# Causal mask in the stack rows, maxima of a batch in one round, transposed scores four units later: two transformer layers with expert stages on one core

## The reference

```python
scores = jnp.einsum('bhqd,bhkd->bhqk', q, k) / jnp.sqrt(jnp.float32(D))
causal = jnp.tril(jnp.ones((T, T), dtype=bool))
scores = jnp.where(causal, scores, -jnp.inf)
weights = jax.nn.softmax(scores, axis=-1)
out = jnp.einsum('bhqk,bhkd->bhqd', weights, v)
```

## Time and profile before

| what | value |
|---|---|
| median of 3 runs | 541.39 us (540.93 to 545.23) |
| the profiled execution | 542.69 us, span 541.0 us |
| TensorE busy | 458.8 us, 85% |
| VectorE, ScalarE, GpSimd busy | 324.4, 247.3, 203.2 us |
| mean granted clock of TensorE | 0.938 |
| steps 1 and 2 | 34.4 to 75.8 us |
| layer-0 experts | 75.8 to 111.4 us |
| steps 3 to 11 | 111.4 to 298.7 us |
| steps 12 and 13 | 298.7 to about 364 us |
| layer-1 experts | about 370 to 449.9 us |
| steps 14 to 18 | 449.9 to 541 us |

### The profile page before, as it was taken

One profiled execution on the slowest core, in us unless ns is written; L12 is line 12 of the kernel. 1 busy time (PEld: TensorE's weight loads), 2 busy tenths in 40 slices (PEclk: granted clock), 3 DMA queues, 4 the chain that ended last, 5 costly groups with the idle time before them and its releaser, 6 DMA issues.

```text
span 541.0 us, 10168 instructions
## 1 busy us (share of the span) xinstructions
PE 458.8 (85%) x3431; PEld 344.6 (64%) x3431; DVE 324.4 (60%) x974; ACT 247.3 (46%) x564; POOL 203.2 (38%) x274
## 2 busy tenths in 40 slices
PE   1668899979899999989989965787999997978874
PEld 1645667656777877767656634456999995654442
DVE  5475631135777877778868964314666664564952
ACT  1821545535555564555445522323555554434542
POOL 6620110004335435435444366870000001767761
PEclk9999999989999999999999977866999998888968
DMA  5642224644314313202357120312222201322130
GB/s 157 155 123 62 71 52 119 189 116 120 94 33 122 110 37 99 76 6 79 124 113 228 46 75 28 124 44 64 60 59 80 73 23 35 107 67 81 35 90 21
DMA packets 51441, 45.89 MB, mean 85 GB/s; under 512 B 4968, under 2 KB 46464, under 8 KB 51392
## 3 DMA queue, kind: packets, MB, share of 16 engines
q1 hardware_dynamic: 47424, 35.54, 23.4%
q0 software_dynamic: 2240, 4.53, 3.1%
q10 hardware_dynamic: 1728, 5.20, 3.0%
HBM read 26.24 MB, written 19.01 MB: 84 GB/s over the span
## 4 chain that ended last, share of the span: by engine, by line
PE 57%; POOL 16%; DVE 8%; issue 8%; DMA 5%; ACT 5%; SPq 1%; ACTq 0%; POOLq 0%; DVEq 0%
PE ps_S L1493 6%; POOL xs L741 6%; PE ps_N L1468 5%; PE ps_N L1658 5%; PE ps_P L1512 5%; POOL PT L688 4%; PE ps_N L1464 4%; PE ps_P L1668 3%; PE ps_M L1709 3%; PE ps_M L1668 3%; PE ps_S L1658 2%; PE ps_M L1555 2%; PE ps_M L1592 2%; POOL XN L750 2%; POOL LATE L750 2%
## 5 line engine op out<-in xcount | busy, mean ns | idle before, releaser
L823 ACT ACTIVATE PT<-ps_S 128x512 f32<-128x512 f32 x192 | 112.3, 591 | 109.2 <-PE ps_S L1493 87.7
L1058 DVE TENSOR_REDUCE NM<-ps_N 128x2 f32<-128x512 f32 (+1 forms) x192 | 127.9, 682 | 51.3 <-PE ps_N L1468 40.0
L688 POOL TENSOR_SCALAR_AFFINE_SELECT PT<-PT 128x512 f32<-128x512 f32 x128 | 78.6, 639 | 172.6 <-ACT PT L823 171.9
L1468 PE MATMUL ps_N<-STK 96*128 96x256 f32 (+1 forms) x256 | 105.7, 456 | 0.0
L1493 PE MATMUL ps_S<-STK 100*128 100x128 f32 (+5 forms) x352 | 88.1, 327 | 17.1 <-ACT PT L823 13.5
L1493 PEld LDWEIGHTS ps_S<-STK 104*128 104x128 f32 (+1 forms) x352 | 62.3, 200 | 25.0 <-ACT PT L823 17.9
L1464 PE MATMUL ps_N<-maskb,identb 128*128 128x256 bf16 (+1 forms) x192 | 63.5, 331 | 11.4 <-issue 8.3
L1512 PE MATMUL ps_P<-PT,VA 128*32 128x256 f32 (+1 forms) x1024 | 59.7, 351 | 7.3 <-POOL PT L688 6.8
L1468 PEld LDWEIGHTS ps_N<-STK 96*128 96x128 f32 x256 | 53.4, 208 | 4.7 <-issue 0.7
L1512 PEld LDWEIGHTS ps_P<-PT,VA 128*32 128x32 f32 x1024 | 28.1, 114 | 36.8 <-issue 15.0
L730 POOL TENSOR_TENSOR ROT<-ROT 128x256 f32<-128x256 f32 (+1 forms) x16 | 11.3, 728 | 97.1 <-DVE ROT L1087 97.1
(11 more groups left out here) (195 smaller groups left out, 811.4 us busy)
## 6 DMA issues: line engine op xcount, KB each, us to landing
STK<-scr SPq DMA_DIRECT2D x96, 96.0 KB
scr<-XQ SPq DMA_DIRECT2D x24, 256.0 KB
ROT<-in_L_ffn_W SPq DMA_DIRECT2D x16, 256.0 KB, 3.0
EW<-in_moe ACTq DMA_DIRECT2D x8, 512.0 KB, 3.6
scr<-XQ SPq DMA_DIRECT2D x24, 128.0 KB
xs<-zero SPq DMA_DIRECT2D x1, 2496.0 KB, 11.1
LATE<-xs SPq DMA_DIRECT2D x9, 256.0 KB, 2.9
ysl<-LATE SPq DMA_DIRECT2D x9, 256.0 KB, 2.3
```

The source lines that it names most:

```text
L688: last = pool.affine_select(out=v, in_=v, compare_op=ALU.is_ge, fill=0.0, base=0, pattern=[[0, 4], [1, P]], channel_multiplier=-1)
L823: act.activation(PT[:, g, r, :], bank[s][:], ACT.Exp, scale=SCALE).then_inc(exp_ok, 1)
L1058: dve.tensor_reduce(NM[b % 2][:, h, qt, :].rearrange("q (p c) -> q c p", p=2)[:, slots[0]:slots[-1] + 1, :], bank[s][:].rearrange("q (c p ...
L1468: last = mm(s[:, 2 * w_ * i:2 * w_ * (i + 1)], stk[0:QK_ROWS, c, P * qt:P * (qt + 1)], stk[0:QK_ROWS, k_slots(L, c, 2 * h, 2), 0:w_], star ...
```

## The change

1. *Mask.* The natural scores no longer get a mask product. The key side of partitions 104 to 125 holds powers of two and the query side negative ones, so that the product of partitions 0 to 127 adds a large negative number wherever key is above query in the diagonal block (`CO_KM`, `CO_QM`; blocks of `MBLK` = 6 tokens). `constant_rows` writes partitions 96 to 127 of both sides with five activations a stack. A unit of the last 128 queries is now two matmuls (keys 0 to 127 over 96 rows, keys 128 to 255 over 128 rows). Since partitions 96 to 103 now take part in the natural product, they have to be zero on the query side when a stack is reused: SyncE copies zeros there, a ninth DMA of the load.
2. *Maxima.* `mxt`, `max_high`, `max_low`, `mrow` work once on 16 heads instead of twice on 8.
3. *Order.* `ST_AT` = 4: the transposed scores of batch c start in unit 4 of their step and reach into units 0 to 3 of the next. The other items move with them.

```diff
-WARM = [(), ()]
 QK_ROWS, ST_ROWS = 96, 104
+MBLK = 6
...
-        t[QK_ROWS + 2 * r:QK_ROWS + 2 * r + 2, CO_SEL + r] = 1.0
+        t[[QK_ROWS + r, QK_ROWS + 4 + r], CO_SEL + r] = 1.0
...
+    for i in range(P):
+        for j in range(-(-P // MBLK)):
+            row, at = ST_ROWS + j, i % MBLK
+            if i // MBLK == j:
+                t[row, [CO_KM + i, CO_KM + P + i]] = 2.0 ** (22 * at - 107)
+                if at < MBLK - 1:
+                    t[row, [CO_QM + i, CO_QM + P + i]] = -2.0 ** (103 - 22 * at)
+            elif i // MBLK < j:
+                t[row, [CO_QM + i, CO_QM + P + i]] = -2.0 ** 124
...
+            early = t == 0
+            if u == (0 if early else 2):
                 add("qk", a)
+            if a and u == (0 if early else 2 + a[0]):
                 add("hi", a)
-            if a and u == a[0]:
+            if a and u == (0 if early else 3 + a[0]):
                 add("lo", a)
...
-            add("st", c, u // 3, u % 3)
+            s, v = (c, u - ST_AT) if u >= ST_AT else (d, u + 12 - ST_AT)
+            add("st", s, v // 3, v % 3)
             add("max", b, u)
-            add("exp", c, u // 3, u % 3)
-            if u % 3 == 2:
-                add("msk", c, u // 3)
+            add("exp", s, v // 3, v % 3)
+            if v % 3 == 2:
+                add("msk", s, v // 3)
...
             if u == 0:
-                add("pv", d, 3)
+                add("mxt", c)
+                add("mrow", c)
+                add("pv", d, 0)
             if u == 1:
-                add("mxt", c, 1)
-                add("mrow", c, 1)
-                add("stack", a)
-                add("ocp", d, 1)
+                add("pv", d, 1)
             if u == 2:
-                add("val", a)
+                add("ocp", d, 0)
             if u == 3:
+                add("pv", d, 2)
+            if u == 4:
+                add("pv", d, 3)
+            if u == (1 if early else 5):
+                add("stack", a)
+            if u == (2 if early else 5):
+                add("val", a)
+            if u == 5:
+                add("ocp", d, 1)
+            if u == (3 if early else 6):
                 add("vev", a)
+            if u == 7:
                 add("otr", d)
                 add("norm", d)
...
-            if u == 5:
-                add("ott", d)
-                layer1("po", e)
-            if u == 6:
-                add("oev", d)
-                add("mxt", b, 0)
-                add("mrow", b, 0)
             if u == 7:
-                add("proj", d)
+                layer1("po", e)
             if u == 8:
-                add("res", d)
-                add("pv", c, 0)
...
             if u == 9:
-                add("pv", c, 1)
+                add("ott", d)
...
             if u == 10:
-                add("ocp", c, 0)
+                add("oev", d)
                 layer1("pl", e)
             if u == 11:
-                add("pv", c, 2)
+                add("proj", d)
+                add("res", d)
...
-            def ones_rows(i):
+            def constant_rows(i):
 
-                act.activation(STK[i][QK_ROWS:ST_ROWS, KS:, :].rearrange("x (c r) t -> x c r t", r=4),
-                               K[QK_ROWS:ST_ROWS, None, CO_SEL:CO_SEL + 4, None].broadcast_to((ST_ROWS - QK_ROWS, 4, 4, T)), ACT.Copy)\
-                    .then_inc(ones_ok, 1)
+                act.activation(STK[i][QK_ROWS:P, 0:KS, :], K[QK_ROWS:P, None, CO_QM:CO_QM + T].broadcast_to((P - QK_ROWS, KS, T)),
+                               ACT.Copy)
+                for r in range(4):
+                    last = act.activation(STK[i][QK_ROWS:P, KS:, :].rearrange("x (c r) t -> x r c t", r=4)[:, r],
+                                          K[QK_ROWS:P, None, CO_KM:CO_KM + T].broadcast_to((P - QK_ROWS, 4, T)), ACT.Identity,
+                                          bias=K[QK_ROWS:P, CO_SEL + r:CO_SEL + r + 1])
+                last.then_inc(ones_ok, 1)
...
-                sp.dma_start(scm[L][b][h], MS[h][:].bitcast(F32)).then_inc(scm_w[h], 16)
-                sp.wait_ge(scm_w[h], 16 * (seq(L, b) + 1))
-                for p in range(2):
-                    r = 2 * h + p
...
+                sp.dma_start(scm[L][b].rearrange("s h t -> h s t"), MS[:].bitcast(F32)).then_inc(scm_w, 16)
+                sp.wait_ge(scm_w, 16 * (n + 1))
+                sp.dma_start(STK[n % NSTK][QK_ROWS:ST_ROWS, 0:KS, :].bitcast(F32),
+                             scm[L][b].rearrange("s (r c) t -> (s r) c t", c=KS)).then_inc(m_in[n % NSTK], 16)
...
-                mm(diag, identb[:], maskb[:, None, :].broadcast_to((P, many, P)), start=True, stop=False,
-                   skip_group_check=True)
                 stk = STK[seq(L, b) % NSTK]
+                q, k = slice(P * qt, P * (qt + 1)), slice(w_ - P, w_)
                 for i, c in enumerate(slots):
-                    last = mm(s[:, 2 * w_ * i:2 * w_ * (i + 1)], stk[0:QK_ROWS, c, P * qt:P * (qt + 1)],
-                              stk[0:QK_ROWS, k_slots(L, c, 2 * h, 2), 0:w_], start=False, stop=True, skip_group_check=True)
+                    o = s[:, 2 * w_ * i:2 * w_ * (i + 1)].rearrange("q (h k) -> q h k", h=2)
+                    if qt > 0:
+                        mm(o[:, :, 0:P], stk[0:QK_ROWS, c, q], stk[0:QK_ROWS, k_slots(L, c, 2 * h, 2), 0:P], start=True, stop=True)
+                    last = mm(o[:, :, k], stk[:, c, q], stk[:, k_slots(L, c, 2 * h, 2), k], start=True, stop=True)
```

99 lines of the change are left out of this document (47 added, 52 removed).

## The result

The changed kernel takes **579.52 us** (median of 4 executions, 576.76 to 581.15) against 541.97 us for the kernel before: a ratio of 1.068 (95% interval 1.061 to 1.074). Slower by 6.8%, where 535 us, and at most 549 us, was forecast. The profiled execution took 576.76 us, 34.1 us above that of before, with a mean granted clock of 0.864 instead of 0.938. Ratios leave out single executions that took far longer than the others, such as 1,025.68 us in experiment 3 and 593.35 us in experiment 9.

What follows compares the result with a forecast made beforehand. TensorE was taken to set the pace in steps 3 to 11, GpSimd from 460 to 521 us. Terms summed to -6.1 us, giving 536.6 (profiled execution) or 535.3 (median): 535 us forecast, range 524 to 549.

Steps and rivals of the forecast that it cites:

- rival 3: Clock falls in every second-layer step, at PV group 3 of steps 8 to 12: 550 us (547 to 554), chance 0.15.
- (a): TensorE's wait before the transposes of the normalised rows, behind the combine, in each step: 1.5 us.
- Clock: Clock drop behind the new 2.6 us waits in the second layer, half of four steps at 1.2 us each: +2.5 us.
- Steps 5 to 7: First-layer steps: 19.9 us each against 19.5, the 2.0 us saved spent on waits: +1.0 us.
- 8 to 11: Second-layer steps: 22.4 us each against 21.25, with a longer wait before PV group 3: +4.6 us.
- (c): TensorE's wait before PV group 3, on exponential and selects: 0.85 us in the first layer, 2.6 in the second.
- (b): TensorE's wait before the transposes of the maxima, for the last row maximum queued behind the logits on VectorE: 1.3 us.
- Mask products: TensorE's work per step without mask products and with two transposes of maxima instead of four: 2.0 us less.
- Steps 3 and 4: Earlier first natural product in step 3, no wait for maxima in step 4; 17.4 and 19.9 us: -6.3 us.
- Gathers and tail: From the first gather in step 14 to the end: earlier and shorter gathers, longer tail (-1.8 - 5.3 + 5.8): -1.3 us.
- Rival 2: Maxima come late at the first transposed unit, 0.5 us in each of 13 steps: 541.5 us (537 to 546), chance 0.22.
- Rival 4: Split natural product exposes its second weight load, 8 in each of 11 steps: 18 us, giving 553 us, chance 0.03.

Runs made afterwards that it cites:

- experiment 3: Changed kernel with 9 unread products filling only the wait before the transposes of the normalised rows: 571.09 us, ratio 1.049 to the kernel before.
- experiment 9: Kernel before, in its own order, with the mask product left out and the natural product of the last 128 queries split in two: 543.00 us, ratio 1.003.
- experiment 4: Same kernel as experiment 3 (changed kernel, only the wait before the transposes of the normalised rows filled), run once for its profile: 571.21 us.
- experiment 1: Changed kernel with unread products filling the waits before the transposes of the normalised rows and before PV group 3, nothing moved: 554.53 us, ratio 1.020.
- 2: Changed kernel with the mask products back in the natural scores, all else as changed: 580.87 us, ratio 1.070 to the kernel before.
- 11: The mended kernel with the mask products back in the natural scores: 541.20 us, ratio 0.999 to the kernel before.
- 12: The mended kernel with 5 unread products ahead of the transposes of the normalised rows: 529.02 us, ratio 0.978 to the kernel before.
- 6: Changed kernel with combine moved to unit 6, transposes of the normalised rows to 10, router logits to 11: 556.57, 567.83, 570.80 and 558.05 us.
- 7: Changed kernel with ScalarE's copy of rotated rows moved to unit 4, PV group 3 to 5, output copy to 6: 552.08 us, ratio 1.023.
- 8: The mended kernel: changed kernel with the moves of both 6 and 7: 531.41 us, ratio 0.982 to the kernel before.
- 10: The mended kernel with transposes of the normalised rows back in unit 9 and logits in 10: 550.04 us, ratio 1.015 to the kernel before.

## Why the prediction was wrong

The mechanism was in the text, as rival 3; its place and its weight were not. Steps 4 to 11 carry the proof, since three kernels with the same order (the change, only (a) filled, both filled) differ there in nothing but the products that fill the waits, and in the clock.

| steps | forecast | full clock | with the drops |
|---|---|---|---|
| 4 to 7 | 4 x 19.9 = 79.6 | 87.6 (experiment 4) | 95.5 |
| 8 to 11 | 4 x 22.4 = 89.6, clock +2.5 | 98.1 (experiment 1) | 109.8 |

205.3 us instead of 171.7: 16.5 us too little for the chains, and 19.6 us of clock where 2.5 stood. Rival 3's sign came true (a clock of 0.83 in steps 8 to 11, where it asked for under 0.90), its time of 547 to 554 us did not.

- **"Clock": this step failed.** It put the drop only behind PV group 3 in the second layer and counted half of four steps. In the trace of before, 1.42 us had left the clock alone and 2.25 us had not the earlier trace rows; I treated everything below 2.25 as safe, with nothing between the two to show it, and gave the forecast waits of 1.5 us no share. Wait (a) came out at 1.91 us, and the drop came in steps 4 to 7 too, and twice in step 8. Rival 3 had the length of a drop right, by luck: its 6.9 us was the length of the stretch at 0.65, of which 4.8 us were at the low level, while the drop itself, from 456.9, lasted 6.8 us. Its cost was too high (half of it, 3.4 us, where experiment 4 shows 2.0 in layer 0), and the places too few: 5, where the changed kernel has 13 between 140 and 360 us. The rule of the Trainium skill that stood beside it (TensorE: Matmul & The Clock Gate, "What's actually happening": the throttled state is the default, and activity releases it) would have made it the main case, had each wait been taken for a pause, and 550 us is still 30 too low. The traces here agree with the rule, by 0.864 on the page and by the fillers, which are activity and nothing else.
- **"Steps 5 to 7" and "8 to 11": right waits, sizes too small.** (a) 1.91 us, not 1.5: from the combine's end to the transposes it is 161.39 to 165.60 = 4.2 us, not 3.5. The normalisations take 1.40 us beside GpSimd's selects, where they took 0.59; without these 0.8 us the chain would be the 3.4 us forecast and the wait 1.1. (c) 1.44 us, not 0.85; in layer 1 3.17, not 2.6: from projection to PV group 3 it is 8.1 us (222.02 to 230.09) and not 7.1, of which 0.9 are two selects that took 2.13 us instead of 1.22. (b) showed as 0.6 to 0.8 us once the clock was up (experiment 4), hidden in the change. All terms were worked out from the kernel before with each link at its bare duration. About 2 us a step are missing; rows of VectorE and GpSimd that got longer side by side are some 1.1 us of it in layer 0 (0.8 in (a), 0.3 in (c)) and 1.5 to 1.7 in layer 1, the rest is hand-overs and queueing.
- **"Mask products", 2.0 us a step: nearly right as work, wrong as time.** A unit of the last queries takes 0.24 us only behind another pair of score products (152.27 to 152.52); most take 0.32 (161.39 to 161.71), but start that much earlier behind their predecessor. In the same place of a step, 159.42 to 161.97 before became 159.90 to 162.24 in experiment 9, over two such units: 0.1 us each, as forecast. One of the first queries saves 0.15 and not 0.22 us (157.99 to 158.31 for the new one). But as time it came to nothing in two orders (2, 9) and to 10 us in 13 steps in the third (11).
- **"Start", "Step 1", "Step 2": more gained** (9.3 us instead of 5.6), and differently: the start came 0.5 us earlier, not 1.0 later, step 1 brought 5.0 us instead of 2.0, step 2 3.7 instead of 4.6.
- **"Steps 3 and 4", -6.3: mostly lost.** They brought -1.7. Wait (a) is there from step 4 on, with its drop, and step 3 has a wait of 2.08 us for a stack load, with a drop behind it. "The stack load: 0" was wrong in that step.
- **"Step 12 up to the first scatter: 0": wrong**, +6.8 us: a wait before PV group 3 of 2.53 us (339.07), one of 1.29 us for VectorE before the next (342.89), the drop behind them, and the end of the drop behind step 11's wait (a).
- **"Gathers and tail": -1.3 forecast**, -2.8 - 1.4 + 8.7 = +4.5 measured, with a clock of 0.79 in the tail.
- **Rival 2** (the maxima late at the first transposed unit) did not come: the waits on that DMA are 0.92 us in the whole trace. **Rival 4** (the second weight load of the split product exposed) did not bring its 18 us, but its sign is half there: the two halves start 0.12 us apart in a few units (152.27 and 152.40) and 0.20 or more in most (161.39 and 161.59).

That the waits cause the drops is shown, by filling (1, 4, 12), by moving (6, 7, 8) and by the reverse (10). Which of the shorter waits has a drop behind it and which has not stays open: one of 0.76 us had one (1), one of 1.44 (4), four of five of 1.16 to 1.18 (9), six of eight of 1.7 (10), none of three of 1.64 (1). So does where the other 13 us in experiment 1's layer-1 steps go link by link; the mended kernel shows only that the order can take most of them back. That VectorE's and GpSimd's rows get longer because they run side by side is read from the rows; no run tested it.

## What to carry to other kernels

Work that is taken off an engine turns into time only where that engine sets the pace; where it turns into idle time of TensorE, it can cost more than it saved, since the clock falls behind the wait. So when a change shortens TensorE's work or shifts its order, list every wait that it opens, price it with a drop as well unless the trace shows many of its length without one, at up to half the drop (here 2.0 us for one of 6.8 in layer 0), in every step in which it stands, and move the consumer a unit later or the producer a unit earlier before judging the edit itself. Products that nobody reads, put into the wait, are a cheap test of whether the clock is to blame; in the changed kernel they brought back 25 us. And look for rows of VectorE and GpSimd that now run side by side: a chain worked out from their old durations can come out too short.
